# Cross-attention and expert FFN on one core: scores and exponentials in one ring of nine pieces, evacuations two pieces ahead, attention loops written out

## What is computed

```python
c = layernorm(x)
s = (c @ w_c + b_c)[:, None] + (q @ w_q + b_q)[None, :] + einsum('cd,qd,d->cq', c, q, w_cq) + b_cq   # 1024 x 6404
a = softmax(s, axis=1)
c2q = a @ q
b_att = softmax(max(s, axis=1)); q2c = b_att @ c
x = x + concat([c, c2q, c * c2q, c * q2c]) @ W_l.T + b_l
# then: x = x + FFN of the expert (one of 8) that the router picks for each row of layernorm(x)
```

## Time and profile before

| | us |
|---|---|
| median of 3 runs | 275.74 |
| the three runs | 275.59, 275.74, 278.57 |
| span of the profiled execution, first to last instruction | 277.8 |

### The profile page before, as it was taken

How to read it: one execution, slowest core, us unless ns; L and a number is a source line. 1 busy time by engine, 2 the same in 40 slices (tenths; PEclk the granted TensorE clock), 3 DMA queues, 4 the chain that set the end, 5 groups by cost and what they waited for, 6 DMA issues and landing times.

```text
span 277.8 us, 5155 instructions
## 1 busy us (share of the span) xinstructions
PE 202.6 (73%) x1661; PEld 143.8 (52%) x1662; DVE 191.0 (69%) x404; ACT 155.9 (56%) x244; POOL 109.8 (40%) x88
## 2 busy tenths in 40 slices
PE   0249489799779979899898995899540039788960
PEld 0113136556546756576566664799440029566850
DVE  2996967948967979889799798978643013465360
ACT  3299176695568569599595994891100016445430
POOL 2369991942901603507116069400004600424233
PEclk9999978979959999999999999899855556999797
DMA  6992079969968999999989989498001261111000
GB/s 252 391 347 79 0 229 179 250 135 204 249 165 153 226 236 228 247 226 252 255 211 261 235 198 214 113 227 146 0 0 38 104 182 48 43 29 43 10 22 0
DMA packets 129245, 44.64 MB, mean 161 GB/s; under 512 B 107927, under 2 KB 127023, under 8 KB 129231
## 3 DMA queue, kind: packets, MB, share of 16 engines
q1 hardware_dynamic: 128216, 42.87, 65.0%
q0 software_dynamic: 864, 1.58, 1.7%
q10 hardware_dynamic: 150, 0.00, 0.0%
HBM read 14.15 MB, written 4.01 MB: 65 GB/s over the span
## 4 chain that ended last, share of the span: by engine, by line
PE 40%; DVE 21%; issue 19%; ACT 8%; DMA 6%; POOL 3%; ACTq 1%; DVEq 0%; POOLq 0%
ACT Pf L564 5%; DVE S L702 5%; PE psS L922 5%; PE psO L937 4%; PE psS L923 4%; PE psS L924 4%; PE psX L937 4%; DVE Phl L720 3%; DMA PT<-Phl 3%; POOL rows_by_expert L502 2%; PE psS L1111 2%; PE psO L940 2%; DVE qTl L691 2%; DVE c_sb L666 2%; PE psX L940 2%
## 5 line engine op out<-in xcount | busy, mean ns | idle before, releaser
L702 DVE TENSOR_SCALAR_CACHE_REDUCE S<-psS 128x1024 f32<-128x1024 f32 (+1 forms) x56 | 61.8, 1105 | 23.7 <-PE psS L924 15.2
L564 ACT ACTIVATE Pf<-S,negb 128x1024 f32<-128x1024 f32 (+1 forms) x56 | 59.1, 1055 | 33.6 <-DVE negb L711 33.6
L720 DVE TENSOR_TENSOR Phl<-Pf,Phl 128x1024 f16<-128x1024 f32 x41 | 58.8, 1433 | 1.3 <-ACT Phl L580 1.3
L922 PE MATMUL psS<-qTh,gh 128*128 128x512 f16 (+1 forms) x104 | 42.0, 404 | 22.5 <-DVE S L702 9.3
L580 ACT CAST Phl<-Pf 128x1024 f16<-128x1024 f32 x48 | 50.2, 1046 | 10.1 <-DMA PT<-Phl 8.0
L447 POOL TENSOR_TENSOR Phl<-Pf,Phl 128x1024 f16<-128x1024 f32 x7 | 15.6, 2226 | 75.8 <-ACT Phl L580 75.8
L923 PE MATMUL psS<-qTl,gh 128*128 128x512 f16 (+1 forms) x104 | 41.8, 402 | 0.0
L924 PE MATMUL psS<-qTh,gl 128*128 128x512 f16 (+1 forms) x104 | 41.7, 401 | 0.0
L937 PE MATMUL psO<-qn,PT 128*128 128x256 f16 x204 | 39.7, 287 | 0.0
L940 PE MATMUL psO<-qn,PT 128*128 128x128 f16 x204 | 37.8, 228 | 0.0
L937 PE MATMUL psX<-qn,PT 128*128 128x256 f16 x204 | 37.5, 278 | 0.0
(11 more groups left out here) (182 smaller groups left out, 394.5 us busy)
## 6 DMA issues: line engine op xcount, KB each, us to landing
stageT<-in_w SPq DMA_DIRECT2D x8, 512.0 KB, 4.4
stageT<-in_ctxT SPq DMA_DIRECT2D x6, 512.0 KB, 6.6
PT<-in_ctx SPq DMA_DIRECT2D x6, 512.0 KB, 6.8
rows_by_expert<-stageT SPq DMA_DIRECT2D x5, 385.5 KB, 3.5
S<-rows_by_expert SPq DMA_DIRECT2D x1, 967.5 KB, 5.5
S<-rows_by_expert SPq DMA_DIRECT2D x15, 64.0 KB, 1.8
PT<-Phl SPq DMA_TRANSPOSE x48, 3.9
Pf<-in_x SPq DMA_DIRECT2D x1, 512.0 KB, 4.0
```

Of the source, the lines that this page charges most:

```text
L564: nc.scalar.activation(Pf[:, e % 3, 0:b - a], S[:, a:b], ACT.Exp, bias=negb[:, bass.ds(t, 1)], accum_out=Lp[:, bass.ds(t * NG + e, 1)]).th ...
L702: nc.vector.tensor_scalar(out=S[:, a:b], in0=psS[n % 3][:, 0:b - a], scalar1=1.0 / GS, scalar2=None, op0=ALU.mult, op1=ALU.max, accum_out= ...
L720: nc.vector.tensor_tensor(lo, Pf[:, e % 3, 0:hi.shape[1]], hi, ALU.subtract).then_inc(low_done, 1)
L922: nc.tensor.matmul(dst, g_h, qTh[:, a:b], start=True, stop=False)
```

## The change

One buffer `S` of nine pieces takes the place of `S` (seven pieces) and `Pf` (three): piece e of block t lives in place (7t + e) modulo 9, and ScalarE takes the exponential in place. An evacuation therefore waits for the low part of nine pieces before, in place of the exponential of seven before, and the exponential waits for no low part. In step t, VectorE does evacuations 0 and 1 of block t + 1 first, then `low(t, e)` followed by evacuation e + 2; `row_max` comes right after evacuation 6, ahead of `low(t, 5)` and `low(t, 6)`. The loops of TensorE, VectorE and ScalarE are written out. TensorE's order is as before. GpSimd's and SyncE's too.

```diff
-        S = sb("S", [P, Q])
-        Pf = sb("Pf", [P, 3, GR])
+        S = sb("S", [P, SLOTS, GR])
...
+        def slot(t, e):
+
+            return S[:, (t * NG + e) % SLOTS, 0:cols(e, GR)[1] - e * GR]
...
-                if e >= 3:
-                    wait_low(act, t, e - 3)
-                elif not isinstance(t, int) or t > 0:
-                    wait_low(act, t - 1, (NG - 1, 4, 5)[e])
-                nc.scalar.activation(Pf[:, e % 3, 0:b - a], S[:, a:b], ACT.Exp, bias=negb[:, bass.ds(t, 1)],
-                                     accum_out=Lp[:, bass.ds(t * NG + e, 1)]).then_inc(exp_done, 1)
+                nc.scalar.activation(slot(t, e), slot(t, e), ACT.Exp, bias=negb[:, t:t + 1],
+                                     accum_out=Lp[:, t * NG + e:t * NG + e + 1]).then_inc(exp_done, 1)
...
-            with act.Fori(1, T - 1) as t:
-                step(t, True)
+            for t in range(T):
+                for e in range(NG):
+                    exp_piece(t, e)
+                    high(t, e)
...
-                if has_prev:
-                    dve.wait_ge(exp_done, (u - 1) * NG + n + 1)
-                    if n == 0:
-                        dve.wait_ge(negb_ready, u)
+                past = u * NG + n - SLOTS
+                if past >= 0:
+                    wait_low(dve, past // NG, past % NG)
+                if u > 0 and n == 0:
+                    dve.wait_ge(negb_ready, u)
...
-            step(0, 0, False, True)
-            dve.wait_ge(row_term_in_psum, 1)
-            nc.vector.tensor_copy(row_term[:, :], psX[:, 0:T]).then_inc(row_term_ready, 1)
-            with dve.Fori(1, T - 2, 2) as t:
-                step(t, 1, True, True)
-                step(t + 1, 0, True, True)
+            for t in range(T - 1):
+                scores(t + 1, 0)
+                scores(t + 1, 1)
+                for e in range(NG):
+                    if e == LAG and t > 0:
+                        attended(t - 1, (t - 1) % 2)
+                    low(t, e)
+                    if e + 2 < NG:
+                        scores(t + 1, e + 2)
+                        if e + 2 == NG - 1:
+                            row_max(t + 1)
+                if t == 0:
+                    dve.wait_ge(row_term_in_psum, 1)
+                    nc.vector.tensor_copy(row_term[:, :], psX[:, 0:T]).then_inc(row_term_ready, 1)
...
-            with pe.Fori(1, T - 2, 2) as t:
-                step(t, 1, True, True)
-                step(t + 1, 0, True, True)
+            for t in range(T - 1):
+                if t == 1:
+                    pe.wait_ge(row_term_ready, 1)
+                    pe.wait_ge(late_gl_ready, 1)
+                for e in range(NG):
+                    if t == 0 and e == LAG:
+                        row_terms()
+                    for c in range(2 * e, min(2 * e + 2, NCH)):
+                        scores(t + 1, c)
+                    if e >= LAG:
+                        weighted(t, e - LAG)
+                    elif t > 0:
+                        weighted(t - 1, NG - LAG + e)
```

More of the change, by code:

```diff
@@ L303, in wait_low @@
         def wait_low(eng, t, e):
-            if isinstance(t, int) and t == T - 1:
+            if t == T - 1:
                 eng.wait_ge(low_done, t * len(LOW_DVE) + e + 1)
@@ L576, in high @@
                     act.wait_ge(pT_landed[e - 3], 16 * (t + 1))
-                elif has_prev:
+                elif t > 0:
                     act.wait_ge(pT_landed[e + 3], 16 * t)
                 _, hi, _, _ = piece(e)
-                nc.scalar.copy(hi, Pf[:, e % 3, 0:hi.shape[1]]).then_inc(high_done, 1)
-            def step(t, has_prev):
+                nc.scalar.copy(hi, slot(t, e)).then_inc(high_done, 1)
+            for t in range(T):
                 for e in range(NG):
                     exp_piece(t, e)
-                    high(t, e, has_prev)
-            step(0, False)
-            with act.Fori(1, T - 1) as t:
-                step(t, True)
-            for e in range(NG):
-                exp_piece(T - 1, e)
-                high(T - 1, e, True)
-                if e == 2:
-                    act.wait_ge(nM_ready, 1)
-                    nc.scalar.activation(eb[:, :], Mrow[:, :], ACT.Exp, bias=nM[:, :],
-                                         accum_out=es1[:, :]).then_inc(eb_ready, 1)
+                    high(t, e)
+                    if t == T - 1 and e == 2:
+                        act.wait_ge(nM_ready, 1)
+                        nc.scalar.activation(eb[:, :], Mrow[:, :], ACT.Exp, bias=nM[:, :],
+                                             accum_out=es1[:, :]).then_inc(eb_ready, 1)
             act.wait_ge(eb_ready, 1)
@@ L707, in row_max @@
                 dve.wait_ge(scores_out, (u + 1) * NG)
-                nc.vector.tensor_reduce(out=mx[:, bass.ds(u, 1)], in_=mxp[:, :], axis=AX.X,
-                                        op=ALU.max).then_inc(max_parts, 1)
+                nc.vector.tensor_reduce(out=mx[:, u:u + 1], in_=mxp[:, :], axis=AX.X, op=ALU.max).then_inc(max_parts, 1)
                 dve.wait_ge(max_parts, u + 1)
-                nc.vector.tensor_scalar(negb[:, bass.ds(u, 1)], mx[:, bass.ds(u, 1)], -1.0, LIFT,
+                nc.vector.tensor_scalar(negb[:, u:u + 1], mx[:, u:u + 1], -1.0, LIFT,
                                         ALU.mult, ALU.add).then_inc(negb_ready, 1)
             def low(t, e):
-                if e in LOW_POOL and not (isinstance(t, int) and t == T - 1):
+                if e in LOW_POOL and t < T - 1:
                     return
@@ L731, in attended @@
                 dve.wait_ge(o_small, 3 * t + 3)
-                nc.vector.scalar_tensor_tensor(out=a_sb[:, bass.ts(t, D)], in0=psA[odd][:, D:2 * D], scalar=Li[:, :],
-                                               in1=otmp[:, :], op0=ALU.mult, op1=ALU.add).then_inc(o_out, 1)
-            def step(t, odd, has_prev, has_next):
-                for e in range(NG):
-                    if e == LAG and has_prev:
-                        attended(t - 1, 1 - odd)
-                    if has_next:
-                        scores(t + 1, e, True)
-                    low(t, e)
-                if has_next:
-                    row_max(t + 1)
+                nc.vector.scalar_tensor_tensor(out=a_sb[:, t * D:(t + 1) * D], in0=psA[odd][:, D:2 * D],
+                                               scalar=Li[:, :], in1=otmp[:, :], op0=ALU.mult,
+                                               op1=ALU.add).then_inc(o_out, 1)
             for n in range(NG):
@@ L952, in row_terms @@
                 last.then_inc(row_term_in_psum, 1)
-            def step(t, odd, has_prev, has_next):
-                for e in range(NG):
-                    if not has_prev and e == LAG:
-                        row_terms()
-                    if has_next:
-                        for c in range(2 * e, min(2 * e + 2, NCH)):
-                            scores(t + 1, c, True)
-                    if e >= LAG:
-                        weighted(t, odd, e - LAG, has_prev)
-                    elif has_prev:
-                        weighted(t - 1, 1 - odd, NG - LAG + e, True)
             pe.wait_ge(g_ready, 2)
@@ L1040, in _ @@
             nc.tensor.transpose(psS[1][0:1, 0:P], m1[:, :], idf[:, :]).then_inc(m1T_in_psum, 1)
-            weighted(T - 2, 0, 3, True)
+            weighted(T - 2, 3)
             pe.wait_ge(m2_ready, 1)
@@ L1055, in _ @@
                 .then_inc(q2c_in_psum, 1)
-            weighted(T - 1, 1, 0, True)
-            weighted(T - 1, 1, 1, True)
+            weighted(T - 1, 0)
+            weighted(T - 1, 1)
             turn_a(2)
             linear_c(0)
-            weighted(T - 1, 1, 2, True)
-            weighted(T - 1, 1, 3, True)
+            weighted(T - 1, 2)
+            weighted(T - 1, 3)
             linear_a(2)
@@ L1064, in _ @@
             for e in (4, 5, 6):
-                weighted(T - 1, 1, e, True)
+                weighted(T - 1, e)
             turn_x2(0)
```

61 lines of the change are left out of this document (30 added, 31 removed).

## The result

The changed kernel takes 292.89 us (median of 4 runs, 291.24 to 297.14) beside 275.66 for the kernel before (median of 4, 272.67 to 278.57): a ratio of 1.0644, 95% interval 1.0521 to 1.0766. The forecast was 279.5, range 273.5 to 285.0. The direction was right, the size was not: +17.2 us instead of +3.75. The ratios here are of fast runs only: one slow run of each kernel, 278.57 before and 297.14 after, is left out of this one. The profiled execution took 292.59, span 290.9. The profiled executions differ by 14.0 us (292.59 and 278.57), their spans by 13.1; the rest of the 17.2 is mostly that the profiled run of before lay 2.9 us above its median.

The account below looks back on a forecast made before the run. Neither TensorE (73% busy) nor VectorE (69%) was taken as a plain bound. Steady steps 3.2, steps 0 to 2 -0.6, tail 0.3 and clock 0.85 sum to +3.75 us: 279.5 us on the median, range 273.5 to 285.0.

Parts of the forecast that it names:

- Direction and chain: Whole kernel: slower by 3.75 us, through a chain of waits from evacuation 1 to evacuation 6 in each steady step.
- the four steady steps: Attention steps 3 to 6: each becomes 18.6 us against 17.77, +0.8 four times, +3.2 us.
- Its DMA lands 3.6 later, at 10.05: Steady step: `low` 0 ends at 6.45, its transpose lands at 10.05, and `high` 3, needing that buffer, starts at 10.1.
- `low` 4 waits for GpSimd, 0.85 us: Steady step, ahead of evacuation 6: GpSimd's weight instruction delays VectorE's `low` 4 by 0.85 us, bounds 0 and 2.1.
- The rival of no hold: Steady steps: GpSimd leaves `low` 4 free, steps stay 17.7 us, early steps slightly shorter, 275.0 us; chance 0.20.
- the third rival: Step starts: TensorE is the bound, evacuation 6 no longer waits, six steps each give back 1.18, 268.7 us; chance 0.08.
- Evacuation 5 at 13.8, a tie with TensorE: Steady step: evacuation 5 waits for GpSimd's `low` 3 (13.8) and TensorE's piece 5 (13.75), so starts at 13.8.
- Steps 0 to 2, -0.6: First three attention steps: +1.2 us around step 0, -1.3 in step 1, -0.5 in step 2, together -0.6.
- Tail, +0.3: After the attention steps: `low` 5 and 6 stand ahead of the first row maximum, +0.3 us, bounds -1 and +1.5.
- Clock, +0.85: Step starts: TensorE's wait of 2.0 us may lower its clock; half of one 1.7 us loss, +0.85, bounds 0 and 6.8.
- the second rival: Steady step starts: the clock falls at every one, +1.7 us for each of four steps, 285.5 us; chance 0.15.
- Instruction fetch, 0: Written-out loops' added instruction fetch priced 0; as a rival, fetches delay transposes, +2 on the forecast, 281.5 us, chance 0.12.

Follow-up runs that it names:

- aligned: The changed kernel with an unused buffer of 260 floats after `S`, so `Phl` and `PT` start on multiples of 256 bytes: 287.51 us, ratio 1.0342.
- ring, loops and old order, aligned: The changed kernel with VectorE's old order and an unused buffer of 260 floats after `S`: 277.85 us, ratio 0.9996.

## Why the prediction was right or wrong

- *Direction and chain: right.* The kernel became slower, and along the path the forecast names. Evacuation 1, `low` 0, transpose 0, `high` 3, GpSimd's `low` 3, evacuation 5, `attended`, `low` 4, evacuation 6: each waits for the one named. Evacuation 5 starts 0.13 us behind GpSimd's `low` 3 (154.57 against 152.31 + 2.13), `low` 4 takes 1.95, `low` 5 is beyond the split, TensorE's wait is 1.76 where 2.0 was said, ScalarE idles ahead of `high` 3. In its own terms the sum came out so (spans): the four steady steps +12.2 us, where 3.2 and 0.85 for the clock were said; steps 0 to 2 -0.1 for -0.6; the tail +2.7 for +0.3; the start -1.7, which no term had.
- *"Its DMA lands 3.6 later, at 10.05": the failed step.* It took one landing of the old order and let the DMA start when `low` 0 ended; by the same landing time transposes 3 and 4 would have been in time for TensorE, which waited 0.9 to 1.7 us for one of them in steps 4, 5 and 6. Measured: transpose 0 issued 1.0 us late behind two entries of SyncE's queue, landing after 5.1 us. The two make `high` 3 start 2.5 us late, and 2.2 us of it reach the step's end; with the splits' hold this is the step of 20.84. Some of the 2.2 would have come without it: aligned, transpose 0 landed 4.2 us after its issue, and evacuation 5 is still 1.1 us late, for TensorE.
- *The address: not seen at all.* The prediction priced the ring by its waits. The shift of all tiles behind it by 1056 bytes costs 5 us or more (145.9 against 140.6 us for the seven steps, changed kernel and realigned; 1.0226, about 6 us, on the kernel before).
- *`low` 4 waits for GpSimd, 0.85 us: right in kind, and near in size* (1.95 us instead of 1.22; 1.0 us a step with splits and loads taken out, an upper bound). The rival of no hold is refuted. That TensorE is the bound, the third rival, is too: the steps grew.
- *Evacuation 5 at 13.8, a tie with TensorE: too early.* Aligned, it starts at 14.9 (149.46 - 134.53), because TensorE itself waits 0.9 us for transpose 4, and that step takes 19.7 us, the forecast plus 1.1. The prediction let only the transposes of `low` 5 and 6 be late. The one step in which no transpose held up TensorE and `low` 4 was held gave the forecast 18.6.
- *Steps 0 to 2, -0.6: near, but by luck.* Measured -0.1, and aligned -2.5 (60.2 us instead of 62.7). But with VectorE's order untouched and only the loops written out they took 57.8, so neither number is what the new order does there; against ring, loops and old order, aligned (59.7), the new order costs 0.5.
- *Tail, +0.3: mis-sized, +2.7.* From evacuation 6 of block 7 to the first maximum over all blocks it takes 5.17 us (179.89 to 185.06) instead of 3.30 (169.50 to 172.80), since `low` 5 and 6 stand between, `low` 6 held by GpSimd to 2.35 us. The first `low` of block 7 is held too, 3.16 us instead of 1.31, by GpSimd's last split (185.09 to 187.22); where that split ran earlier, all of the loss behind the steps was gone (108.0):

```profile
181.76 2.35 DVE L715 TENSOR_TENSOR Ptail<-S,Ptail 128x260 f16<-128x260 f32 x1
184.04 0.99 DVE L781 TENSOR_TENSOR Mrow<-mx,row_term 128x8 f32<-128x8 f32 x1
...
185.14 3.16 DVE L715 TENSOR_TENSOR Phl<-S,Phl 128x1024 f16<-128x1024 f32 x1
```

- *Clock, +0.85 and the second rival:* not seen in the changed kernel, whose steady steps have clock 1.00 behind waits of up to 1.76 us. Aligned, one steady step behind a wait of 2.30 us had 0.92 and the others 1.00; with the loops alone, two behind 2.10 and 2.45 us had 0.91. So the danger was there and close.
- *Instruction fetch, 0: right for the whole time* (0.9989); within the steps it is not settled, since the one profile with written-out loops has steps 3 to 6 longer by 3.9 us. The rival named the right victim, delayed transposes, but the larger cause is another.
- *The median:* taking the profiled run of before for the slowest was right. But it lay 2.9 us above its median and the profiled run of the changed kernel did not, so the difference of the profiles, 14.0 us, is smaller than that of the medians, 17.2.

## What to carry to other kernels

When a buffer changes size, work out where every tile behind it then starts, and look at the DMA queue's share for the same packets and bytes: if it rises, rule the addresses out before judging the edit. When a wait is moved, follow it through the queue of the engine that issues the DMA and take the landing time under load, not one from a quiet place. Here a two-source read held up by another engine cost little behind the last instruction that the next step waits for, and up to the whole hold ahead of it; making it due sooner only lengthened the hold. Compare with a kernel that differs by one edit, and look at each stretch: two kernels of equal time had steps that differed by a microsecond.

## What the runs showed of the hardware

- Moving the float16 tiles that transposing DMAs read and write from a start on a multiple of 256 bytes to one 224 bytes above it took q1 from 65.0% to 73.2% of about the same span, and the median landing from 3.9 to 4.9 us, with nothing changed but where the tiles behind `Pf` start.
- A VectorE subtraction with two SBUF sources, issued 0.2 us behind the start of a GpSimd subtraction of the same size, took 2.99 us instead of 1.22, and ended 1.08 us behind it; so did one of 1.95 us and, in the tail, one of 3.16. Evacuations from PSUM beside GpSimd kept 1.22.
- Written-out loops raised the instruction queue from 8 to 12 transfers and q1's share from 65.0 to 69.6% with no longer time: a queue's share alone, without the waits behind it, is no verdict.
